# A sparse-attention kernel: turned blocks multiplied by diagonal matrices of reciprocals, a row test and one difference computed by GpSimd

## The chip, the cores and the metric

The kernel runs on one core of a Trainium2 chip. The time is that of one launch on the device in microseconds (us), the median of several runs. PE is TensorE, DVE is VectorE, ACT is ScalarE, POOL is GpSimd, and SP issues the transfers.

## The reference

Input `x` has 16 batches of 512 rows of 128. Each batch goes through attention with 16 heads and 16 extra memory keys, with the heads mixed before and after the softmax and only the 64 largest scores of each row kept, then through a gated feed-forward block. Each of the two has a layer norm ahead, one behind, and a residual addition.

```python
dots = jnp.einsum('bhid,bhjd->bhij', q, k) * scale
dots = jnp.einsum('bhij,hk->bkij', dots, pre_proj)
dots = jnp.where(causal[None, None], neg, dots)
vk = lax.top_k(dots, 64)[0][..., -1:]
dots = jnp.where(dots < vk, neg, dots)
attn = jax.nn.softmax(dots, axis=-1)
attn = jnp.einsum('bhij,hk->bkij', attn, post_proj)
out = jnp.einsum('bhij,bhjd->bhid', attn, v)
x = x + layernorm(out @ Wo + bo)
x = x + layernorm(ffn(layernorm(x)))   # ffn: (silu(x wg) * (x wu)) wd
```

## The kernel before

The weights are multiplied into each other at the start, so that a head needs a score product (`a_all`, `gT`) and a value product (`b_all`, `u_all`) and no output projection. Then one loop runs over the 16 batches and, within a batch, over 16 steps, one head each (`step(s)` on each engine; a first, seven times two middle ones, a last and a drain that finishes what is in flight). A head's 512 rows are four tiles `t` of 128 rows; because of the causal mask tile `t` has 128(t+1) keys, and 16 memory keys, so 144, 272, 400 and 528 columns (`ROW`), 1344 in all.

A head is spread over eight steps. In its own step PE makes the scores and DVE copies them with the row maxima (L1207). In the following steps the 64th largest value of each row is found by guesses: ACT counts per row how many scores lie above a guess (`signs`, L913, three guesses a step), and DVE turns the counts into new guesses (L1120 to L1146, "the moves"; `between` is the difference of two brackets, masked in L1128). Four steps on, DVE counts above the last guess (`found`, L1073), POOL subtracts what is above (L1355), DVE takes the eight largest of the rest (`max`, L1087), and `offset` (POOL, L1336: ranks plus `found`) picks the right one, reduced to `kth` (L1095). `spread` and `missed` (L1102, L1107) test whether the last guess was so far off that this doesn't hold for some row; PE sums `missed` over the rows into `flag_part`, DVE copies it to `flags` (L1070), and where it is above zero DVE does the slow selection `general_kth`. Six steps on, DVE makes `probs` (exponentials at or above `kth`, L1188) with their row sums and the reciprocals `rinv` (L1193), POOL multiplies `probs` by them (L1347) and copies the memory columns to `pmem` (L1362), PE turns the blocks of 128 x 128 (L783, ten a head), ACT copies them out (`probsT`, L924), and a step later PE multiplies them with the values into `y_bank` (L770).

The order on each engine is that of the code, written by hand; engines meet at semaphores. The waits that matter here: POOL's `offset` of a step waits for `kth` of the same step of DVE (`kth_ready`), because it overwrites what the reduce reads; POOL's scaling waits for `rinv` of the same step; PE's turning waits for `scaled`. Steps 1, 8, 9 and 15 have a layer norm on POOL behind `offset` (`extras`, L1256 to L1275), steps 0, 7, 8 and 14 its statistics on DVE behind L1207, step 10 maxima of memory scores, and steps 11 to 13 the gate of the feed-forward block (`f_up`) on DVE behind the moves.

## Time and profile before

| | |
|---|---|
| median of 3 runs | 3364.86 us (3363.4 to 3366.53) |
| the profiled execution | 3363.66 us, span 3361.9 us |
| its mean granted TensorE clock | 0.903 of 2.4 GHz |
| DVE, ACT busy | 88%, 86% of the span |
| PE, POOL busy | 80%, 56% |
| transfers | 22.66 MB, mean 7 GB/s |

The span is first to last instruction of the profiled execution. "Busy" counts instructions that compute, and one that overlaps the end of the one ahead is not counted twice in it. Where the profile gives the start of two instructions on one engine, their distance says what the first costs that engine, waits included; the duration also has the part that overlaps the next. A wait is put down to the instruction whose semaphore came last.

### The profile page before, as it was taken

To read this page: it belongs to the slowest core of one execution; us is meant where nothing else is said; L and a number is where in the kernel's file an instruction comes from. 1 tells how busy PE (TensorE), PEld (TensorE's weight loads), DVE (VectorE), ACT (ScalarE), POOL (GpSimd) and SP (SyncE) were. 2 spreads that over 40 slices of the span, in tenths; PEclk is the share of its full clock that TensorE was granted. 3 is DMA by queue.
4 is the path that set the end of the run, shared out by engine and by line. 5 is a ranking of instruction groups with operands and counts; after the bars stand their busy time and mean duration, and the time that the engine had idled before them with its cause. 6 is when DMAs were issued, how large, how long until landed. Compare 5 with 4: busy or idle time off the path is not lost. (4 is left out here: it accounts for less than half of the span.)

```text
span 3361.9 us, 70684 instructions
## 1 busy us (share of the span) xinstructions
PE 2675.5 (80%) x13754; PEld 1771.9 (53%) x13754; DVE 2958.5 (88%) x12547; ACT 2891.6 (86%) x8666; POOL 1887.2 (56%) x3623
## 2 busy tenths in 40 slices
PE   7878888888877888888787867887788887888765
PEld 3455555555545555555555545555455555555543
DVE  4599999999989999999999989998999999998985
ACT  1699989898978989999898978989899898989972
POOL 3455566555655555566565546655565665555543
PEclk8989899898988998999999888989899899999977
DMA  1000000000000000000000000000000000000000
GB/s 44 7 2 2 5 8 5 9 2 5 8 5 9 2 9 5 5 9 5 8 2 11 2 5 8 3 11 2 5 8 5 9 2 11 2 5 9 2 8 4
DMA packets 31404, 22.66 MB, mean 7 GB/s; under 512 B 3201, under 2 KB 30338, under 8 KB 30722
## 3 DMA queue, kind: packets, MB, share of 16 engines
q1 hardware_dynamic: 30722, 16.03, 1.7%
q14 instruction: 555, 4.55, 0.4%
q8 instruction: 127, 2.08, 0.3%
HBM read 11.83 MB, written 4.19 MB: 5 GB/s over the span
## 5 line engine op out<-in xcount | busy, mean ns | idle before, releaser
L913 ACT ACTIVATE signs<-scores,state 128x528 int8<-128x528 f32 (+3 forms) x3072 | 1723.5, 574 | 74.7 <-DVE state L1146 74.2
L1347 POOL TENSOR_SCALAR probs<-probs,rinv 128x528 f32<-128x528 f32 (+3 forms) x1024 | 538.9, 545 | 1300.6 <-DVE rinv L1193 1300.6
L783 PE MATMUL t_bank<-ident,probs 128*128 128x128 f32 x2560 | 485.5, 334 | 601.9 <-POOL probs L1347 593.6
L1355 POOL TENSOR_TENSOR work<-scores,work 128x528 f32<-128x528 f32 (+3 forms) x1024 | 888.3, 900 | 11.6 <-DVE work L1073 11.6
L759 PE MATMUL s_bank<-xn,gT 128*128 128x512 f32 (+3 forms) x2048 | 761.8, 496 | 1.8 <-ACT gT L844 0.7
L783 PEld LDWEIGHTS t_bank<-ident,probs 128*128 128x128 f32 x2560 | 325.7, 164 | 708.6 <-issue 582.5
L770 PEld LDWEIGHTS y_bank<-u_all,probsT 128*128 128x128 f32 x5120 | 616.8, 194 | 109.4 <-issue 98.8
L770 PE MATMUL y_bank<-u_all,probsT 128*128 128x128 f32 x5120 | 625.4, 278 | 6.6 <-ACT probsT L924 6.5
L924 ACT COPY probsT<-t_bank 128x512 f32<-128x512 f32 (+1 forms) x768 | 400.5, 522 | 251.2 <-PE t_bank L783 247.6
L913 ACT ACTIVATION_READ_ACCUMULATOR signs<-scores,state 128x1 f32 x3072 | 614.7, 200 | 0.0
L1073 DVE TENSOR_SCALAR_CACHE_REDUCE work<-scores,state 128x528 f32<-128x528 f32 (+3 forms) x1024 | 531.1, 553 | 46.2 <-DVE state L1146 46.2
L934 ACT ACTIVATE expo<-scores,negmax 128x528 f32<-128x528 f32 (+3 forms) x1024 | 542.2, 590 | 0.0
L1188 DVE SCALAR_TENSOR_TENSOR probs<-scores,kth,expo 128x528 f32<-128x528 f32 (+3 forms) x1024 | 520.9, 565 | 9.1 <-issue 6.1
L1207 DVE TENSOR_SCALAR_CACHE_REDUCE scores<-s_bank,memmax 128x512 f32<-128x512 f32 (+3 forms) x1024 | 516.5, 543 | 5.9 <-PE s_bank L761 5.7
L759 PEld LDWEIGHTS s_bank<-xn,gT 128*128 128x128 f32 x2048 | 358.1, 210 | 286.2 <-issue 276.2
L1087 DVE MAX8 state<-work 128x8 f32<-128x528 f32 (+3 forms) x1024 | 441.5, 491 | 0.2 <-issue 0.2
L631 PE MATMUL misc<-b_all,xn 128*128 128x512 f32 x512 | 301.4, 673 | 9.2 <-ACT u_all L844 9.2
L668 PE MATMUL misc<-xn,a_all 128*128 128x512 f32 x512 | 264.3, 598 | 6.0 <-DVE f_up L1162 6.0
L761 PE MATMUL s_bank<-causal,ident 128*128 128x128 bf16 x1024 | 228.5, 223 | 0.0
L761 PEld LDWEIGHTS s_bank<-causal,ident 128*128 128x128 bf16 x1024 | 105.7, 103 | 128.2 <-issue 91.0
L844 ACT COPY u_all<-misc 128x512 f32<-128x512 f32 x256 | 148.9, 582 | 8.5 <-PE misc L631 8.5
L844 ACT COPY gT<-misc 128x512 f32<-128x512 f32 x256 | 151.8, 593 | 0.9 <-PE misc L668 0.9
(156 smaller groups left out, 2984.0 us busy)
## 6 DMA issues: line engine op xcount, KB each, us to landing
xwork<-in_L_attn_x_dram SPq DMA_DIRECT2D x17, 256.0 KB, 2.8
xres<-in_L_attn_x_dram SPq DMA_DIRECT2D x16, 256.0 KB, 2.9
out_dram<-ybuf SPq DMA_DIRECT2D x16, 256.0 KB, 2.4
u_all<-in_L_attn_Wq_dram SPq DMA_DIRECT2D x1, 512.0 KB, 3.5
u_all<-in_L_attn_Wk_dram SPq DMA_DIRECT2D x1, 512.0 KB, 4.4
u_all<-in_L_attn_Wv_dram SPq DMA_DIRECT2D x1, 512.0 KB, 5.3
u_all<-in_L_attn_Wo_dram SPq DMA_DIRECT2D x1, 512.0 KB
expo<-in_L_ffn_w_gate_dram SPq DMA_DIRECT2D x1, 192.0 KB, 4.7
```

Source lines behind the costliest of these rows:

```text
L759: nc.tensor.matmul(score_part(t, 0, KEYS[t]), lhsT=gT[s % 2][:, t * P:(t + 1) * P], rhs=xn[par][:, 0:KEYS[t]], start=True, stop=False, ski ...
L770: mm = nc.tensor.matmul(y_bank[:, t * P:(t + 1) * P], lhsT=probsT[:, h % 2, at:at + P], rhs=u_all[:, j, h * D:(h + 1) * D], start=False, s ...
L783: mm = nc.tensor.transpose(t_bank[q % 2][:, at:at + P], probs[:, h % 2, KEY_AT[t] + j * P:KEY_AT[t] + (j + 1) * P], ident[:, :])
L913: nc.scalar.activation(signs[:, k, AT[t]:AT[t] + ROW[t]], row(scores, ring(head_of(s, k + 1), RING), t), ACT.Sign, bias=guesses(s % STATES ...
L924: nc.scalar.copy(probsT[:, h % 2, PART_AT[q]:PART_AT[q + 1]], t_bank[q % 2][:, 0:PART_AT[q + 1] - PART_AT[q]]).then_inc(t_taken, 1)
L934: nc.scalar.activation(row(expo, ring(head_of(s, LAG_E), ERING), t), row(scores, ring(head_of(s, LAG_E), RING), t), ACT.Exp, bias=negmax[: ...
L1073: v.tensor_scalar(work[:, s % 2, AT[t]:AT[t] + ROW[t]], row(scores, slot_k, t), guessed[:, t:t + 1], None, ALU.is_ge, ALU.add, accum_out=f ...
L1087: v.max(candidates(past)[:, t, 1:9], work[:, s % 2, AT[t]:AT[t] + ROW[t]]).then_inc(select_step, 1)
L1188: v.scalar_tensor_tensor(out=probs[:, slot_p % 2, AT[t]:AT[t] + ROW[t]], in0=row(scores, slot_p, t), scalar=kth[:, bass.ds(slot_p, 1), t], ...
L1207: v.tensor_scalar(keys(scores, slot, t), score_part(t, 0, KEYS[t]), 1.0, memmax[par][:, t, bass.ds(s, 1)], ALU.mult, ALU.max, accum_out=ro ...
L1347: nc.gpsimd.tensor_scalar(prb, prb, rinv[:, slot_p, t:t + 1], 1.0, ALU.mult, ALU.mult).then_inc(scaled, 1)
L1355: nc.gpsimd.tensor_tensor(wrk, row(scores, slot_k, t), wrk, ALU.subtract).then_inc(hidden, 1)
```

## The change

Four things change.

- POOL no longer multiplies `probs` by `rinv`. It multiplies the identity by it, one 128 x 128 matrix `diag[:, t, :]` for each tile, and PE's turn becomes a real matrix product with that diagonal as moving operand, which turns and scales the block at once. `pmem` gets its factor in POOL's copy, now a multiplication with two inputs. The scaling waits for PE's previous turn (`t_full`).
- `spread` and `missed` are made by POOL, from two more columns of `offset` (11 for each tile, `found` less the aim plus and minus the reach), as a product and a comparison with 0. DVE's two instructions go.
- The sum of `missed` over the tiles is no longer made with `missed`; DVE's copy of `flags` adds up instead (an instruction with an accumulator).
- The bracket difference `between` is made by POOL at the end of these, and DVE waits for it (`between_ready`) ahead of L1128.

```diff
@@ PE, turn @@
-                        mm = nc.tensor.transpose(t_bank[q % 2][:, at:at + P],
-                                                 probs[:, h % 2, KEY_AT[t] + j * P:KEY_AT[t] + (j + 1) * P], ident[:, :])
+                        mm = nc.tensor.matmul(t_bank[q % 2][:, at:at + P],
+                                              lhsT=probs[:, h % 2, KEY_AT[t] + j * P:KEY_AT[t] + (j + 1) * P],
+                                              rhs=diag[:, t, :], start=True, stop=True, skip_group_check=True)
@@ DVE @@
-                        v.tensor_copy(flags[:, :], flag_part).then_inc(flag_taken, 1)
+                        v.tensor_scalar(flags[:, 0:T], flag_part, 1.0, None, ALU.mult, ALU.add,
+                                        accum_out=flags[:, T:T + 1]).then_inc(flag_taken, 1)
...
-                    if checks:
-                        number = found[:, (s - 1) % 2, :]
-                        dve.wait_ge(found_ready, 4 * ge + 4)
-                        alone(dve)
-                        v.scalar_tensor_tensor(out=spread[:, :], in0=number, scalar=-2.0 * AIM, in1=number,
-                                               op0=ALU.add, op1=ALU.mult).then_inc(select_step, 1)
-                        dve.wait_ge(select_step, 1)
-                        at_least(dve, flag_full, ge)
-                        alone(dve)
-                        v.scalar_tensor_tensor(out=missed[:, 0:T], in0=spread[:, :], scalar=WINDOW ** 2 + 0.5 - AIM ** 2,
-                                               in1=active, op0=ALU.is_gt, op1=ALU.mult,
-                                               accum_out=missed[:, T:T + 1]).then_inc(bad_ready, 1)
...
-                        v.tensor_tensor(between[:, :, :], pair(past, S_T, -1), pair(last, S_OTHER, 0),
-                                        ALU.subtract).then_inc(guess_step, 1)
...
+                        dve.wait_ge(guess_step, 2)
+                        dve.wait_ge(between_ready, g - 1)
+                        alone(dve)
                         v.scalar_tensor_tensor(out=between[:, :, :],
@@ POOL @@
-                        nc.gpsimd.tensor_tensor(offset[:, :, 0:9], ranks,
-                                                found[:, (s - 1) % 2, :].unsqueeze(2).to_broadcast([P, T, 9]),
+                        nc.gpsimd.tensor_tensor(offset[:, :, 0:11], ranks,
+                                                found[:, (s - 1) % 2, :].unsqueeze(2).to_broadcast([P, T, 11]),
                                                 ALU.add).then_inc(offset_ready, 1)
+                        ge = g - LAG_E
+                        pool.wait_ge(offset_ready, ge + 1)
+                        alone(pool)
+                        nc.gpsimd.tensor_tensor(spread[:, :], offset[:, :, 0:1].squeeze(2), offset[:, :, 1:2].squeeze(2),
+                                                ALU.mult).then_inc(spread_ready, 1)
+                        pool.wait_ge(spread_ready, ge + 1)
+                        at_least(pool, flag_full, ge)
+                        alone(pool)
+                        nc.gpsimd.tensor_scalar(missed[:, :], spread[:, :], 0.0, 1.0, ALU.is_gt, ALU.mult).then_inc(bad_ready, 1)
+                    if any(lagged(kind, s, k + 2) for k in range(GUESSES)):
+                        last, past = (s - 1) % STATES, (s - 2) % STATES
+                        at_least(pool, guess_ready, g - 2)
+                        at_least(pool, first_ready, g - 1 if lagged(kind, s, 2) else 0)
+                        alone(pool)
+                        nc.gpsimd.tensor_tensor(between[:, :, :], pair(past, S_T, -1), pair(last, S_OTHER, 0),
+                                                ALU.subtract).then_inc(between_ready, 1)
                     extras(kind, b, s)
                     gp, slot_p = g - LAG_P, head_of(s, LAG_P) % 2
                     if lagged(kind, s, LAG_P):
                         pool.wait_ge(rinv_ready, gp + 1)
                         at_least(pool, probs_ready, 4 * gp + 4)
+                        at_least(pool, t_full, 3 * gp)
                         alone(pool)
                         for t in SCORE_ORDER:
-                            prb = probs[:, slot_p, AT[t]:AT[t] + ROW[t]]
-                            nc.gpsimd.tensor_scalar(prb, prb, rinv[:, slot_p, t:t + 1], 1.0, ALU.mult,
+                            nc.gpsimd.tensor_scalar(diag[:, t, :], ident[:, :], rinv[:, slot_p, t:t + 1], 1.0, ALU.mult,
                                                     ALU.mult).then_inc(scaled, 1)
...
-                        pool.wait_ge(scaled, 4 * gp + 4)
                         alone(pool)
-
-                        nc.gpsimd.tensor_copy(head_mem(pmem, head_of(s, LAG_P)), mem_parts(probs[:, slot_p, :])).then_inc(pmem_ready, 1)
+                        shares = rinv[:, slot_p, :].rearrange("p (a t) -> p a t", a=2).unsqueeze(3)
+                        nc.gpsimd.tensor_tensor(head_mem(pmem, head_of(s, LAG_P)).rearrange("p a t m -> p a t m"),
+                                                mem_parts(probs[:, slot_p, :]), shares.to_broadcast([P, 2, 2, M]),
+                                                ALU.mult).then_inc(pmem_ready, 1)
```

On POOL, from the last subtraction of one step to the scaling of the next, in a middle batch. Before:

```order
L1355 TENSOR_TENSOR work<-scores,work 128x144 [waits found_ready]
L1362 COPY pmem<-probs 128x4x16 [waits scaled]
L1312 ISA
L1315 TENSOR_TENSOR negmax<-rowmax,minus_unit 128x4 [waits masked]
L1321 COPY state<-seed 128x2x4 [waits guess_ready]
L1330 COPY scores<-smem 128x2x32 [waits probs_ready]
L1336 TENSOR_TENSOR offset<-consts,found 128x4x9 [waits kth_ready,found_ready]
L1347 TENSOR_SCALAR probs<-probs,rinv 128x528 [waits rinv_ready,probs_ready]
```

And now, the same place:

```order
L1365 TENSOR_TENSOR work<-scores,work 128x144 [waits found_ready]
L1371 TENSOR_TENSOR pmem<-probs,rinv 128x4x16
L1306 ISA
L1309 TENSOR_TENSOR negmax<-rowmax,minus_unit 128x4 [waits masked]
L1315 COPY state<-seed 128x2x4 [waits guess_ready]
L1324 COPY scores<-smem 128x2x32 [waits probs_ready]
L1330 TENSOR_TENSOR offset<-consts,found 128x4x11 [waits kth_ready,found_ready]
L1336 TENSOR_TENSOR spread<-offset 128x4 [waits offset_ready]
L1341 TENSOR_SCALAR missed<-spread 128x4 [waits spread_ready,flag_full]
L1347 TENSOR_TENSOR between<-state 128x24 [waits guess_ready,first_ready]
L278 REGISTER_ALU [waits probs_ready,rinv_ready]
L1357 TENSOR_SCALAR diag<-ident,rinv 128x128 [waits t_full]
```

Three instructions stand between `offset` and the scaling that did not stand there, two of them behind waits for the one ahead, and `between` is the last of them.

On DVE, from the choice of the 64th value to the masked bracket, same batch. Before:

```order
L1090 SCALAR_TENSOR_TENSOR offset<-offset,state 128x4x9 [waits select_step,offset_ready]
L1094 ISA [waits select_step]
L1095 TENSOR_REDUCE kth<-offset 128x4
L1102 SCALAR_TENSOR_TENSOR spread<-found 128x4 [waits found_ready]
L1107 SCALAR_TENSOR_TENSOR missed<-spread,consts 128x4 [waits select_step,flag_full]
L1120 TENSOR_TENSOR state<-counts,consts 128x12 [waits first_ready,counted2,counted0,counted1]
L1121 TENSOR_TENSOR between<-state 128x24
L1125 TENSOR_TENSOR product<-state 128x24 [waits guess_step]
L1128 SCALAR_TENSOR_TENSOR between<-product,between 128x24 [waits guess_step]
```

And now:

```order
L1097 SCALAR_TENSOR_TENSOR offset<-offset,state 128x4x9 [waits select_step,offset_ready]
L1101 ISA [waits select_step]
L1102 TENSOR_REDUCE kth<-offset 128x4
L1114 TENSOR_TENSOR state<-counts,consts 128x12 [waits first_ready,counted2,counted0,counted1]
L1117 TENSOR_TENSOR product<-state 128x24 [waits guess_step]
L1122 SCALAR_TENSOR_TENSOR between<-product,between 128x24 [waits guess_step,between_ready]
```

Three instructions are gone between `kth` and the masked bracket, and the latter waits for POOL too.

## Rows read from the trace of the kernel before

**Rows 1.** The page, first part: engine busy us, share, instructions.

```profile
PE 2675.5 (80%) x13754; PEld 1771.9 (53%) x13754; DVE 2958.5 (88%) x12547; ACT 2891.6 (86%) x8666; POOL 1887.2 (56%) x3623
```

**Rows 2.** Who waited for whom: engine, line, releaser, us in total, times, longest.

```profile
POOL probs L1347 <- DVE rinv L1193: 1300.6, 256, 23.0
```

**Rows 3.** DVE in order of time: start us, us, engine, line, operation.

```profile
1515.12 0.18 DVE L1193 RECIPROCAL rinv<-rowsum 128x4 f32<-128x4 f32 x1
...
1520.08 0.20 DVE L1095 TENSOR_REDUCE kth<-offset 128x4 f32<-128x40 f32 x1
1520.19 0.41 DVE L1102 SCALAR_TENSOR_TENSOR spread<-found 128x4 f32<-128x4 f32 x1
...
1521.01 0.23 DVE L1120 TENSOR_TENSOR state<-counts,consts 128x12 f32<-128x12 f32 x1
...
1521.32 0.21 DVE L1125 TENSOR_TENSOR product<-state 128x24 f32<-128x24 f32 x1
1521.56 0.18 DVE L1128 SCALAR_TENSOR_TENSOR between<-product,between 128x24 f32<-128x24 f32 x1
...
1522.84 0.17 DVE L1146 TENSOR_TENSOR state<-state,move 128x12 f32<-128x12 f32 x1
...
1526.49 0.18 DVE L1193 RECIPROCAL rinv<-rowsum 128x4 f32<-128x4 f32 x1
```

**Rows 4.** POOL in order of time, the same step.

```profile
1515.50 2.10 POOL L1347 TENSOR_SCALAR probs<-probs,rinv 128x528 f32<-128x528 f32 x4 [4.91 <-DVE rinv L1193]
1517.57 3.46 POOL L1355 TENSOR_TENSOR work<-scores,work 128x528 f32<-128x528 f32 x4
1520.97 0.24 POOL L1362 COPY pmem<-probs 128x64 f32<-128x64 f32 x1
1521.16 0.20 POOL L1315 TENSOR_TENSOR negmax<-rowmax,minus_unit 128x4 f32<-128x4 f32 x1
...
1521.62 0.25 POOL L1336 TENSOR_TENSOR offset<-consts,found 128x36 f32<-128x36 f32 x1
```

**Rows 5.** Groups by form (POOL) and by line (DVE): count, busy us, mean ns.

```profile
L1347 POOL TENSOR_SCALAR probs<-probs,rinv 128x528 f32<-128x528 f32 x256 | 180.6, 705 | 1300.6 <-DVE rinv L1193 1300.6
...
L1355 POOL TENSOR_TENSOR work<-scores,work 128x144 f32<-128x144 f32 x256 | 125.5, 490 | 0.0
L1347 POOL TENSOR_SCALAR probs<-probs,rinv 128x144 f32<-128x144 f32 x256 | 98.5, 385 | 0.0
...
L1121 DVE TENSOR_TENSOR between<-state 128x24 f32<-128x24 f32 x258 | 53.2, 206 | 0.2 <-issue 0.2
```

**Rows 6.** A step with a normalization, in order of time: DVE, then POOL.

```profile
1644.56 0.20 DVE L1095 TENSOR_REDUCE kth<-offset 128x4 f32<-128x40 f32 x1
...
1645.66 0.22 DVE L1128 SCALAR_TENSOR_TENSOR between<-product,between 128x24 f32<-128x24 f32 x1
...
1646.95 0.95 DVE L1146 TENSOR_TENSOR state<-state,move 128x12 f32<-128x12 f32 x1
...
1649.31 0.77 DVE L1188 SCALAR_TENSOR_TENSOR probs<-scores,kth,expo 128x528 f32<-128x528 f32 x1
...
1644.92 0.24 POOL L1336 TENSOR_TENSOR offset<-consts,found 128x36 f32<-128x36 f32 x1
1645.26 0.25 POOL L1256 TENSOR_SCALAR vareps<-meanvar 128x4 f32<-128x4 f32 x1
1645.65 1.04 POOL L1259 TENSOR_TENSOR rstd<-vareps,minus_half 128x4 f32<-128x4 f32 x1
1646.84 1.04 POOL L1268 TENSOR_TENSOR ybuf<-ybuf,rstd 128x512 f32<-128x512 f32 x1
1648.02 0.73 POOL L1274 TENSOR_TENSOR ybuf<-xres,ybuf 128x256 f32<-128x256 f32 x1
```

**Rows 7.** PE in order of time: products into `y_bank`, then turned blocks.

```profile
1499.29 2.39 PE L770 MATMUL y_bank<-u_all,probsT 128*128 128x128 f32 x20
...
1504.99 0.65 PE L783 MATMUL t_bank<-ident,probs 128*128 128x128 f32 x4 [2.33 <-POOL probs L1347]
```

More of the change, by code:

```diff
@@ L139, in guess_table @@
             table[i, T + t] = (z - FAR / (2 * density)) * UNIT ** 0.5
-            table[i, 5 * T + 9 * T + t] = float(active)
-            table[i, 5 * T + 10 * T + t] = 0.0 if active else -FMAX
+            reach = WINDOW + 0.5 if active else FAR
+            table[i, 5 * T + 11 * t] = reach - AIM
+            table[i, 5 * T + 11 * t + 1] = -reach - AIM
+            table[i, 5 * T + 11 * T + t] = 0.0 if active else -FMAX
         for k in range(GUESSES):
             table[:, 2 * T + k * T + t] = ROW[t] - 2 * AIM - 0.25
-        table[:, 5 * T + 9 * t:5 * T + 9 * t + 9] = np.arange(9) - TOPK
+        table[:, 5 * T + 11 * t + 2:5 * T + 11 * t + 11] = np.arange(9) - TOPK
     return table
@@ L324, in build @@
         centre = sb("centre", [P, P])
+        diag = sb("diag", [P, T, P])
         row_sum = sb("row_sum", [P, 2 * HC])
@@ L342, in build @@
         found = sb("found", [P, 2, T])
-        offset = sb("offset", [P, T, 10])
+        offset = sb("offset", [P, T, 12])
         spread = sb("spread", [P, T])
-        missed = sb("missed", [P, T + 1])
+        missed = sb("missed", [P, T])
         flags = sb("flags", [1, T + 1])
@@ L443, in build @@
         select_step = sem("select_step")
+        spread_ready = sem("spread_ready")
         bad_ready = sem("bad_ready")
+        between_ready = sem("between_ready")
         scaled = sem("scaled")
@@ L1053, in _ @@
             dve.wait_ge(state_set, 3)
-            nc.vector.tensor_copy(offset[:, :, 9:10].squeeze(2), cap)
+            nc.vector.tensor_copy(offset[:, :, 11:12].squeeze(2), cap)
             def batch(kind, b, par):
@@ L1088, in step @@
                         dve.wait_ge(offset_ready, gp + 1)
-                        dve.wait_ge(select_step, T + 1)
-                        v.scalar_tensor_tensor(out=offset[:, :, 0:9], in0=offset[:, :, 0:9], scalar=0.0,
+                        dve.wait_ge(select_step, T)
+                        v.scalar_tensor_tensor(out=offset[:, :, 2:11], in0=offset[:, :, 2:11], scalar=0.0,
                                                in1=candidates(past), op0=ALU.is_equal,
                                                op1=ALU.mult).then_inc(select_step, 1)
-                        dve.wait_ge(select_step, T + 2)
+                        dve.wait_ge(select_step, T + 1)
                         dve.sem_clear(select_step)
-                        v.tensor_reduce(kth[:, bass.ds(slot_p, 1), :].squeeze(1), offset[:, :, :], AX_X,
+                        v.tensor_reduce(kth[:, bass.ds(slot_p, 1), :].squeeze(1), offset[:, :, 2:12], AX_X,
                                         ALU.add).then_inc(kth_ready, 1)
-                    if checks:
-                        number = found[:, (s - 1) % 2, :]
-                        dve.wait_ge(found_ready, 4 * ge + 4)
-                        alone(dve)
-                        v.scalar_tensor_tensor(out=spread[:, :], in0=number, scalar=-2.0 * AIM, in1=number,
-                                               op0=ALU.add, op1=ALU.mult).then_inc(select_step, 1)
-                        dve.wait_ge(select_step, 1)
-                        at_least(dve, flag_full, ge)
-                        alone(dve)
-                        v.scalar_tensor_tensor(out=missed[:, 0:T], in0=spread[:, :], scalar=WINDOW ** 2 + 0.5 - AIM ** 2,
-                                               in1=active, op0=ALU.is_gt, op1=ALU.mult,
-                                               accum_out=missed[:, T:T + 1]).then_inc(bad_ready, 1)
                     if moves:
@@ L1134, in step @@
                                                in1=miss, op0=ALU.is_gt, op1=ALU.mult).then_inc(guess_step, 1)
-                        dve.wait_ge(guess_step, 4)
+                        dve.wait_ge(guess_step, 3)
                         v.tensor_tensor(other, pair(last, S_OTHER, 0), between[:, :, :], ALU.add).then_inc(guess_step, 1)
+                        dve.wait_ge(guess_step, 5)
+                        v.tensor_tensor(apart[:, :, :], pair(last, S_T, 0), other, ALU.subtract).then_inc(guess_step, 1)
                         dve.wait_ge(guess_step, 6)
-                        v.tensor_tensor(apart[:, :, :], pair(last, S_T, 0), other, ALU.subtract).then_inc(guess_step, 1)
-                        dve.wait_ge(guess_step, 7)
                         v.reciprocal(apart[:, 1, :], apart[:, 1, :]).then_inc(guess_step, 1)
                         v.tensor_tensor(move[:, :], apart[:, 0, :], move[:, :], ALU.mult).then_inc(guess_step, 1)
+                        dve.wait_ge(guess_step, 8)
+                        v.tensor_tensor(move[:, :], move[:, :], apart[:, 1, :], ALU.mult).then_inc(guess_step, 1)
                         dve.wait_ge(guess_step, 9)
-                        v.tensor_tensor(move[:, :], move[:, :], apart[:, 1, :], ALU.mult).then_inc(guess_step, 1)
-                        dve.wait_ge(guess_step, 10)
                         dve.sem_clear(guess_step)
```

11 lines of the change are left out of this document (5 added, 6 removed).

## Prediction

> **What bounds the kernel now.** I read the busy shares first, then the waits, then one step of each engine in order of time. The shares [rows 1] put DVE (VectorE) at 88% and ACT (ScalarE) at 86%, POOL (GpSimd) at 56%, PE (TensorE) at 80%. The largest wait is POOL's, for DVE's reciprocals `rinv`, 1300.6 us in 256 times, about 5 us in every step [rows 2]; none of DVE's own waits is among the long ones. So a step is as long as DVE's chain, with ACT close behind: it gains room if DVE's steps get longer, and would hold DVE back soon if they got shorter.
>
> The step that I use runs from `rinv` at 1515.12 to `rinv` at 1526.49, 11.37 us [rows 3]. Three stretches make it up: `rinv` to the reduce that gives `kth` 4.96 (1520.08), `kth` to L1128 1.48 (1521.56), L1128 to the next `rinv` 4.93. POOL's side of that step [rows 4]: it starts 0.38 behind `rinv` (1515.50), scales for 2.07, subtracts (L1355) for 3.40, copies `pmem` 0.19, and reaches `offset` 0.46 after `negmax`, at 1521.62, which is `rinv` + 6.50. It then idles until the next `rinv`.
>
> **What leaves DVE.** `spread` and `missed` go: from `kth` to L1120 it is 0.93 (1520.08 to 1521.01) [rows 3]. `kth` to `spread`, with one pair of waits between, is 0.11; L1120 has one pair more, so I take 0.23 for what stays, a gain of 0.70. `between` (L1121) goes too, but it stood in the shadow of the result that L1125 needs: L1120 to L1125 is 0.31, a dependent pair (L1125 to L1128) 0.24, so about 0.07. The new wait in front of L1128 costs about 0.1, the distance that a further wait takes in front of L1120. `flags` becomes an instruction with an accumulator; the bounds are 0 and 0.24, a dependent pair; I take 0.1, since the old copy and the new one have equally few columns. DVE by itself would gain 0.70 + 0.07 - 0.1 - 0.1, about 0.57 a step. That is what the change is worth if nobody is late.
>
> **What POOL gets, and when.** The place decides. `between` of a step stands on POOL behind `offset`, `spread` and `missed` of the same step, and `offset` waits for `kth` of the same step, since it overwrites what the reduce reads. DVE would come to L1128 at `kth` + 0.79. On the old timing POOL reaches only `offset` at `kth` + 1.54. So DVE will wait there, and POOL's queue is on the path. Its time, from `rinv`:
> - start 0.38.
> - four diagonal blocks of 128 columns in place of 1344 columns. The 528-column form takes 705 ns, the 144-column one 385 [rows 5], 0.83 ns a column; of the 2.07 for all four that leaves 0.24 each, so a block of 128 costs 0.35, the four 1.38. The bounds are 0.24 and 0.39 each. Gain only 0.69, because most of a short instruction is fixed.
> - L1355 unchanged, 3.40.
> - `pmem` with a second input, 64 columns: between the copy's 0.19 and the 0.49 of L1355's 144-column form [rows 5]; I take 0.28, near `offset` (36 columns, 0.25).
> - `negmax` to `offset` 0.46.
>
> `offset` then starts at 0.38 + 1.38 + 3.40 + 0.28 + 0.46 = 5.90. The other bound is DVE: where POOL had to wait for `kth`, `offset` came 0.36 behind it (1644.56, 1644.92) [rows 6], here 4.96 + 0.1 + 0.36 = 5.42. The later one counts, 5.90.
>
> Behind it three more instructions, two of which read the result of the one ahead. The row for such a pair is `vareps` to `rstd`: 0.39 for an instruction of 0.25 [rows 6], so its duration plus 0.14. `offset` 0.27 + 0.14 = 0.41; `spread` as `negmax`, 0.20 + 0.14 and 0.04 for a second wait, 0.38; `missed` to `between` between 0.14 (`negmax` to the next) and 0.34 (`offset` to `vareps`), I take 0.23; `between` 0.23 + 0.14 until DVE goes on, 0.37. Sum 1.39. L1128 starts at `rinv` + 7.29; now it is 6.44. With 4.93 behind it the step is 12.22: **0.85 longer**.
>
> **Two opinions on small work on POOL.** DVE's `between` takes 206 ns [rows 5], POOL's nearest row, `offset` with more columns, 0.25 us. The Trainium skill, page "GPSIMD Engine Reference", section "Engine selection", speaks against this move: elementwise work belongs on VectorE, GpSimd being about twice as slow on two inputs. By that factor, an estimate, `between` on POOL would take 0.41 instead of 0.23 and the whole kernel 46 us more. The rows say that at these sizes the factor is near 1.2, and that place and dependence cost more than the engine's speed.
>
> **The other steps.** A batch has 16 steps. In 11 of them nothing but the above lies between `rinv` and `kth` (with the three that work on `f_up`, which lies elsewhere): 11 x 0.85 = 9.4. In five, DVE has statistics or maxima there, and `kth` is so late that POOL waits for it even today: L1128 comes at `kth` + 0.1 + 0.36 + 1.39 = 1.85, where it was 1.10 (1644.56 to 1645.66) [rows 6]: +0.75. In one (maxima) that is all. In the four whose POOL has a normalization there, a stall goes: L1146 took 0.95 there and 0.17 otherwise, because it ran into POOL's `ybuf` instruction of 1.04 (from 1646.84, `offset` + 1.92). After the change POOL's follows `between` by the same 1.92, L1146 by 0.37 + 1.29 = 1.66, in time. So -0.78. But L1188 then starts at `between` + 3.24 (1646.95 to 1649.31 less the stall is 1.58), into POOL's next instruction, which begins at +3.10: until about 3.7 where it has 256 columns (0.73; two steps), about 4.0 where 512 (1.04; one step). Together 4 x (0.75 - 0.78) + 2 x 0.45 + 0.75 = 1.5. A batch is longer by 9.4 + 0.75 + 1.5 = 11.6, sixteen batches by **186 us**. The profiled execution took 3363.66 (span 3361.9), 1.2 below the median of the three runs; 3363.66 + 186 = 3550, on the median's scale 3551.
>
> **PE and ACT.** A turned block was one matmul; a real product of this type is two: ten blocks of `y_bank` are 20 in 2.39, 0.12 each, four turned ones were 4 in 0.65 [rows 7]. So ten more, 1.2 us a step. Cover: PE was idle for 2.33 before the first turned block, which is more than 1.2. It may also begin 0.33 earlier, as the first block to wait for costs POOL 0.37 (385 less 16 columns) and no longer 0.70; its first four blocks then take 8 x 0.12 = 0.96 and no longer 0.65. ACT, which copies them out, gets them within 0.1 of the old time and has gained 0.85 of room. Price 0; if the cover is gone, as where PE's granted clock is at its lower level, the first four blocks come later by their growth, up to 0.3 a step, 77 us.
>
> **Rivals.**
> - POOL's queue is cheaper than I make it, and only `kth` rules it: `offset` at 5.42, L1128 at 6.81, +0.37 in the 11 steps; 4.1 + 0.75 + 1.5 = 6.3 a batch, +101: 3465. For it: several short instructions are priced from neighbours. Against it: 0.48 us would have to be found in 1.66 of them (the blocks and `pmem`), and their fixed part alone is 1.1.
> - DVE's gain arrives: `between` would have to be ready by `kth` + 0.79, while `kth` + 0.36 + 1.39 is the earliest with every price above. It decides at 1.0 us less, as if POOL did the difference ahead of `offset`. Then 0.57 x 256 = 146 off: 3218. For it: `between` needs nothing from `kth`. Against it: the order of POOL's instructions.
> - It cancels: the wait costs just DVE's gain, 3365. It would need L1128 near `kth` + 1.4, below the same 1.75.
> - PE and ACT come on top: 3550 + 77 = 3627. For it: ACT at 86% and twice the instructions in front of its copies. Against it: the cover above.
>
> **How the numbers follow.** Forecast 0.74, the cheaper queue 0.12, PE and ACT on top 0.08, cancelling 0.02, faster 0.04. A measurement tells 0.2% of this kernel (7 us) from no change. Slower 0.94, same 0.02, faster 0.04. The range takes the two neighbours, 3465 to 3627; the unknown prices (0.11 for the distance to `between`, 0.06 for the blocks, 0.1 for the added wait for `t_full`) make 0.27 a step, 69 us, and stay within it.
>
> **What would show it.** After: POOL's wait for `rinv` still about 5 us a step (4.93 + 0.14 + 0.38 less `between`), so nothing of it is won; a wait of DVE at the masked `between` for POOL's, in nearly every step, of 7.29 - 4.96 - 0.1 - 0.79 = 1.4 us where POOL's queue rules and 1.0 where `kth` does, some 300 us in all; DVE's busy share falling; steps of 12.2. No such wait, or steps under 11.37, makes the prediction wrong; a wait of about 1.0 with steps of 11.7 makes it the cheaper queue.

## The result, and the profile of the changed kernel

| kernel | median us | lowest to highest | ratio to before |
|---|---|---|---|
| before | 3364.19 | 3363.4 to 3366.53 | 1 |
| changed | 3548.22 | 3544.98 to 3551.0 | 1.0545 [1.0527, 1.0564] |

The change costs 184 us; 3551 (3465 to 3627) was predicted. The profiled execution of the changed kernel took 3544.98 us, its span is 3543.2. The page, first part, and then the waits (engine, line, releaser, us in total, times, longest):

```profile
PE 2902.9 (82%) x16314; PEld 2152.0 (61%) x16314; DVE 2808.3 (79%) x11777; ACT 2903.2 (82%) x8666; POOL 1914.3 (54%) x4393
```

```profile
POOL diag L1357 <- DVE rinv L1187: 1339.7, 256, 22.8
...
DVE between L1122 <- POOL between L1347: 356.5, 255, 2.0
...
POOL offset L1330 <- DVE kth L1102: 45.8, 75, 2.2
```

DVE fell from 88% [rows 1] to 79%, and a wait that was not there, of 356.5 us in 255 steps, stands in front of the masked `between`. POOL idles for `rinv` as long as before (1339.7; 1300.6 in [rows 2]). Each engine now waits for the other once a step. DVE in order of time, in the step that answers to [rows 3]:

```profile
1501.02 0.18 DVE L1187 RECIPROCAL rinv<-rowsum 128x4 f32<-128x4 f32 x1
...
1505.60 0.34 DVE L1097 SCALAR_TENSOR_TENSOR offset<-offset,state 128x36 f32<-128x36 f32 x1
1506.07 0.20 DVE L1102 TENSOR_REDUCE kth<-offset 128x4 f32<-128x40 f32 x1
1506.30 0.28 DVE L1114 TENSOR_TENSOR state<-counts,consts 128x12 f32<-128x12 f32 x1
1506.61 0.18 DVE L1117 TENSOR_TENSOR product<-state 128x24 f32<-128x24 f32 x1
1508.32 0.18 DVE L1122 SCALAR_TENSOR_TENSOR between<-product,between 128x24 f32<-128x24 f32 x1 [1.53 <-POOL between L1347]
...
1513.22 0.18 DVE L1187 RECIPROCAL rinv<-rowsum 128x4 f32<-128x4 f32 x1
```

POOL in the same step, to be set beside [rows 4]:

```profile
1501.45 1.41 POOL L1357 TENSOR_SCALAR diag<-ident,rinv 128x128 f32<-128x128 f32 x4 [7.18 <-DVE rinv L1187]
1502.82 3.48 POOL L1365 TENSOR_TENSOR work<-scores,work 128x528 f32<-128x528 f32 x4
1506.26 0.29 POOL L1371 TENSOR_TENSOR pmem<-probs,rinv 128x64 f32<-128x64 f32 x1
1506.51 0.19 POOL L1309 TENSOR_TENSOR negmax<-rowmax,minus_unit 128x4 f32<-128x4 f32 x1
...
1506.99 0.26 POOL L1330 TENSOR_TENSOR offset<-consts,found 128x44 f32<-128x44 f32 x1
1507.39 0.20 POOL L1336 TENSOR_TENSOR spread<-offset 128x4 f32<-128x4 f32 x1
1507.78 0.24 POOL L1341 TENSOR_SCALAR missed<-spread 128x4 f32<-128x4 f32 x1 [0.19 <-POOL spread L1336]
1507.99 0.24 POOL L1347 TENSOR_TENSOR between<-state 128x24 f32<-128x24 f32 x1
```

DVE has its product at 1506.61 and could go on at about 1506.9. POOL reaches `offset` at 1506.99 and needs 1.24 more until `between` is done. DVE goes on at 1508.32, which is `rinv` + 7.30. The step is 12.20 long, where it was 11.37.

### The profile page after: what moved, and what is told of

Read it like the earlier page. It is cut to its first block and busy times, and to the rows that moved or that the text cites. A ratio compares the mean times of both kernels' runs of the same rounds, so it can differ in the third digit from the quotient of the medians.

```text
span 3543.2 us, 76572 instructions
## 1 busy us (share of the span) xinstructions
PE 2902.9 (82%) x16314; PEld 2152.0 (61%) x16314; DVE 2808.3 (79%) x11777; ACT 2903.2 (82%) x8666; POOL 1914.3 (54%) x4393
## 5 line engine op out<-in xcount | busy, mean ns | idle before, releaser
L788 PE MATMUL t_bank<-diag,probs 128*128 128x128 f32 x5120 | 841.8, 334 | 553.2 <-POOL diag L1357 547.9
L788 PEld LDWEIGHTS t_bank<-diag,probs 128*128 128x128 f32 x5120 | 781.2, 240 | 582.7 <-issue 486.6
L1357 POOL TENSOR_SCALAR diag<-ident,rinv 128x128 f32<-128x128 f32 x1024 | 362.5, 374 | 1341.2 <-DVE rinv L1187 1339.7
L764 PE MATMUL s_bank<-xn,gT 128*128 128x512 f32 (+3 forms) x2048 | 688.8, 458 | 0.8 <-ACT gT L850 0.7
L775 PE MATMUL y_bank<-u_all,probsT 128*128 128x128 f32 x5120 | 617.5, 276 | 5.4 <-ACT probsT L930 5.3
L919 ACT ACTIVATION_READ_ACCUMULATOR signs<-scores,state 128x1 f32 x3072 | 601.0, 196 | 0.0
L1182 DVE SCALAR_TENSOR_TENSOR probs<-scores,kth,expo 128x528 f32<-128x528 f32 (+3 forms) x1024 | 554.5, 597 | 26.9 <-issue 18.7
L764 PEld LDWEIGHTS s_bank<-xn,gT 128*128 128x128 f32 x2048 | 329.9, 195 | 238.1 <-issue 230.2
L1122 DVE SCALAR_TENSOR_TENSOR between<-product,between 128x24 f32<-128x24 f32 x258 | 49.1, 190 | 356.9 <-POOL between L1347 356.5
L636 PE MATMUL misc<-b_all,xn 128*128 128x512 f32 x512 | 283.9, 637 | 9.4 <-ACT u_all L850 9.4
```

The lines of the kernel that those rows point to most:

```text
L764: nc.tensor.matmul(score_part(t, 0, KEYS[t]), lhsT=gT[s % 2][:, t * P:(t + 1) * P], rhs=xn[par][:, 0:KEYS[t]], start=True, stop=False, ski ...
L775: mm = nc.tensor.matmul(y_bank[:, t * P:(t + 1) * P], lhsT=probsT[:, h % 2, at:at + P], rhs=u_all[:, j, h * D:(h + 1) * D], start=False, s ...
L788: mm = nc.tensor.matmul(t_bank[q % 2][:, at:at + P], lhsT=probs[:, h % 2, KEY_AT[t] + j * P:KEY_AT[t] + (j + 1) * P], rhs=diag[:, t, :], s ...
L919: nc.scalar.activation(signs[:, k, AT[t]:AT[t] + ROW[t]], row(scores, ring(head_of(s, k + 1), RING), t), ACT.Sign, bias=guesses(s % STATES ...
L1182: v.scalar_tensor_tensor(out=probs[:, slot_p % 2, AT[t]:AT[t] + ROW[t]], in0=row(scores, slot_p, t), scalar=kth[:, bass.ds(slot_p, 1), t], ...
L1357: nc.gpsimd.tensor_scalar(diag[:, t, :], ident[:, :], rinv[:, slot_p, t:t + 1], 1.0, ALU.mult, ALU.mult).then_inc(scaled, 1)
```

## Experiments

In what follows a plain step is one without statistics or maxima ahead of `kth`. Its length is read from two `rinv` rows. Where I give the length of a kind of step over all batches, it is the median over the batches of the distance between two successive `rinv` rows. The experiments ran in three groups, each beside runs of the kernel before of its own (median 3364.42 for e1 to e4, 3359.99 for e5 to e8, 3368.55 for e9 and e10; 3364.19 beside the changed kernel). Where two kernels of different groups are compared, the difference of the ratios is the safer one, and it is given where it differs.

Theory: each part of the change does for DVE what it is meant to do, and the loss comes only from the order on POOL's queue: `offset`, `spread`, `missed` and only then `between`, with DVE waiting for the last. Rivals: each part is slow by itself on POOL; or PE and ACT, with twice the instructions in front of the copies of the turned blocks, hold the step.

### One part at a time

**e1_diag.** The kernel before with the diagonal matrices alone:

```
-  mm = nc.tensor.transpose(t_bank[...], probs[...], ident[:, :])
+  mm = nc.tensor.matmul(t_bank[...], lhsT=probs[...], rhs=diag[:, t, :], ...)
...
-  nc.gpsimd.tensor_scalar(prb, prb, rinv[:, slot_p, t:t + 1], 1.0, ...)
+  nc.gpsimd.tensor_scalar(diag[:, t, :], ident[:, :], rinv[:, slot_p, t:t + 1], 1.0, ...)
...
-  nc.gpsimd.tensor_copy(head_mem(pmem, ...), mem_parts(probs[...]))
+  nc.gpsimd.tensor_tensor(head_mem(pmem, ...), mem_parts(probs[...]), shares..., ALU.mult)
```

> The kernel before with the first part alone: diagonal matrices on POOL, real products on PE, the scaled copy of pmem. The row test and the bracket difference stay on DVE. Theory (the change is slow because DVE waits for POOL's bracket difference): no DVE instruction waits for POOL here, so no loss; POOL's subtraction ends about 0.7 us earlier in a step, so that DVE's spread and missed, stretched to 0.41 and 0.32 beside it in the rows of before, run at 0.16 and 0.22 as in the steps with a normalization: 0.2 to 0.3 us a step less, 3300 to 3355. Rival (the real products cost twice PE's instructions and hold ACT and DVE back): slower than before by up to 0.7 us a step, 3400 to 3545.

Measured: 3321.96 us (3321.17 to 3323.16) beside 3364.42 of before, ratio 0.9869 [0.9853, 0.9886]: 42 us faster, as the theory expected. The plain step is 11.07. Two rows of DVE and one of POOL tell where the gain is:

```profile
1507.88 0.20 DVE L1097 TENSOR_REDUCE kth<-offset 128x4 f32<-128x40 f32 x1
1508.00 0.16 DVE L1104 SCALAR_TENSOR_TENSOR spread<-found 128x4 f32<-128x4 f32 x1
...
1508.07 0.30 POOL L1363 TENSOR_TENSOR pmem<-probs,rinv 128x64 f32<-128x64 f32 x1
```

`spread` takes 0.16 here and took 0.41 in [rows 3]. There POOL's subtractions (from 1517.57 for 3.46, to 1521.03 [rows 4]) still ran when it started at 1520.19. Here POOL's queue is 0.6 us earlier: the last subtraction gives way to `pmem` at 1508.07, 0.07 behind the start of `spread`, and leaves it next to nothing to wait for. The parts of the change touch each other through this: the diagonal matrices give DVE time, though they take nothing off it.

**e2_test.** The kernel before with the row test alone on POOL (table, `offset` with 44 columns, `flags` with an accumulator):

```
-  v.scalar_tensor_tensor(out=spread[:, :], ...)
-  v.scalar_tensor_tensor(out=missed[:, 0:T], ..., accum_out=missed[:, T:T + 1])
...
+  nc.gpsimd.tensor_tensor(spread[:, :], offset[:, :, 0:1]..., offset[:, :, 1:2]..., ALU.mult)
+  nc.gpsimd.tensor_scalar(missed[:, :], spread[:, :], 0.0, 1.0, ALU.is_gt, ALU.mult)
```

> The kernel before with the row test alone moved to POOL (spread and missed behind offset, the sum made by DVE's copy of flags). Theory: nothing on DVE waits for POOL's test, so DVE keeps its gain as far as POOL's subtraction, which now runs beside the moves, and ACT's load let it: between 3240 and 3330. Rival (a longer POOL queue or the accumulating flags copy is what costs): slower than before, above 3375.

Measured: 3299.85 us (3294.62 to 3301.94), ratio 0.9799 [0.978, 0.9818], 65 us faster and within what was expected; DVE does not wait for POOL.

**e3_between.** The kernel before with the difference alone on POOL, right behind `offset`:

```
-  v.tensor_tensor(between[:, :, :], pair(past, S_T, -1), pair(last, S_OTHER, 0), ALU.subtract)
...
+  dve.wait_ge(between_ready, g - 1)
...
+  nc.gpsimd.tensor_tensor(between[:, :, :], pair(past, S_T, -1), pair(last, S_OTHER, 0),
+                          ALU.subtract).then_inc(between_ready, 1)
```

> The kernel before with the bracket difference alone moved to POOL, behind offset, and the wait for it on DVE. Theory: offset starts at rinv + 6.50 as before, the difference 0.33 later, DVE goes on 0.37 after that, at 7.20 where it was 6.44: 0.76 us in 11 of 16 steps, none in the others: 3365 + 134, about 3500 (3460 to 3530), with a DVE wait of 200 us or more at the masked bracket. Rival (the products are the cause): within 20 us of before.

Measured: 3440.82 us (3437.22 to 3442.61), ratio 1.0221 [1.0203, 1.0239]: 76 us slower. The sign is as expected, the size about half, and the time lies below the 3460 to 3530 that were expected. One plain step, DVE and then POOL:

```profile
1526.90 0.20 DVE L1096 TENSOR_REDUCE kth<-offset 128x4 f32<-128x40 f32 x1
...
1528.10 0.26 DVE L1124 TENSOR_TENSOR product<-state 128x24 f32<-128x24 f32 x1
1528.98 0.18 DVE L1129 SCALAR_TENSOR_TENSOR between<-product,between 128x24 f32<-128x24 f32 x1 [0.63 <-POOL between L1345]
...
1528.44 0.25 POOL L1337 TENSOR_TENSOR offset<-consts,found 128x36 f32<-128x36 f32 x1
1528.65 0.25 POOL L1345 TENSOR_TENSOR between<-state 128x24 f32<-128x24 f32 x1
```

I had put 0.33 between `offset` and `between`, the price where the next instruction needs the one ahead; `between` needs nothing of `offset`, and it is 0.21. The steps with a normalization gained besides, since the stall of L1146 [rows 6] went there.

By themselves the three parts give -42, -65 and +76, together -31. The change gives +184. So no part explains the loss by its own cost: 215 us come only when the three are together. That it is their order on POOL's queue, the next runs show.

### The change without the moved difference, and with it elsewhere

**e4_diag_test.** The changed kernel with the difference back on DVE, so the first two parts together:

```
+  v.tensor_tensor(between[:, :, :], pair(past, S_T, -1), pair(last, S_OTHER, 0), ALU.subtract)
...
-  dve.wait_ge(between_ready, g - 1)
...
-  nc.gpsimd.tensor_tensor(between[:, :, :], ...).then_inc(between_ready, 1)
```

> The changed kernel with the bracket difference alone given back to DVE; everything else of the change stays. Theory: the wait goes, DVE gains what its own chain lost, 0.5 us a step less what ACT allows (its own work is about 11.2 us in a step with two extras): 3215 to 3290. Rival (products on PE and ACT cost the time): stays above 3450.

Measured: 3277.58 us (3275.49 to 3281.39), ratio 0.9739 [0.9721, 0.9756]. It beats both kernels, the one before by 87 us. A plain step, DVE and POOL's `offset`:

```profile
1535.97 0.18 DVE L1186 RECIPROCAL rinv<-rowsum 128x4 f32<-128x4 f32 x1
...
1541.04 0.20 DVE L1101 TENSOR_REDUCE kth<-offset 128x4 f32<-128x40 f32 x1
...
1541.80 0.24 DVE L1121 SCALAR_TENSOR_TENSOR between<-product,between 128x24 f32<-128x24 f32 x1
...
1546.79 0.18 DVE L1186 RECIPROCAL rinv<-rowsum 128x4 f32<-128x4 f32 x1
...
1541.97 0.28 POOL L1329 TENSOR_TENSOR offset<-consts,found 128x44 f32<-128x44 f32 x1
```

The masked `between` stands at `rinv` + 5.83, even ahead of POOL's `offset`; in the changed kernel it is at 7.30. The step is 10.82. Moving this one instruction of 206 ns [rows 5] costs the kernel 271 us.

**e5_early.** The changed kernel, POOL's `between` for the next step made right behind the diagonal matrices and ahead of the subtraction; no instruction more or less:

```
   nc.gpsimd.tensor_scalar(diag[:, t, :], ...)
+  nc.gpsimd.tensor_tensor(between[:, :, :], pair(prev, S_T, -1), pair(nxt, S_OTHER, 0),
+                          ALU.subtract).then_inc(between_ready, 1)
   ...
   nc.gpsimd.tensor_tensor(wrk, row(scores, slot_k, t), wrk, ALU.subtract)
```

> The changed kernel with one thing moved: POOL makes the bracket difference of the next step right behind the four diagonal blocks, ahead of its subtraction, in place of behind the row test. Same instructions, same count. Theory (place in POOL's queue and the dependence on kth cost the time, not POOL's speed): DVE finds it ready, waits under 10 us in all, and the time falls to that of the kernel with the difference on DVE (3278), within 3265 to 3310. Rival (POOL is simply given too much): stays above 3400.

Measured: 3309.81 us (3304.45 to 3315.69) beside 3359.99 of before, ratio 0.9852 [0.9835, 0.987]. The place of the instruction alone is worth 238 us (233 by the ratios). DVE no longer waits for it:

```profile
1500.83 0.53 DVE L1097 SCALAR_TENSOR_TENSOR offset<-offset,state 128x36 f32<-128x36 f32 x1
1501.49 0.20 DVE L1102 TENSOR_REDUCE kth<-offset 128x4 f32<-128x40 f32 x1
...
1502.04 0.18 DVE L1117 TENSOR_TENSOR product<-state 128x24 f32<-128x24 f32 x1
1502.36 0.18 DVE L1122 SCALAR_TENSOR_TENSOR between<-product,between 128x24 f32<-128x24 f32 x1
```

But it is still 32 us behind e4, which makes the difference on DVE, and 38 by the ratios (0.9852 against 0.9739). From `kth` to the masked `between` it is 0.87 here and 0.76 in e4: the wait costs more than the instruction in the shadow saved. And L1097 takes 0.53 here; the last two experiments are about that.

**e6_swap.** The changed kernel with `between` right behind `offset` and the test behind it:

```
   nc.gpsimd.tensor_tensor(offset[:, :, 0:11], ranks, ...)
+  nc.gpsimd.tensor_tensor(between[:, :, :], ...).then_inc(between_ready, 1)
   nc.gpsimd.tensor_tensor(spread[:, :], ...)
   nc.gpsimd.tensor_scalar(missed[:, :], ...)
-  nc.gpsimd.tensor_tensor(between[:, :, :], ...).then_inc(between_ready, 1)
```

> The changed kernel with the bracket difference right behind offset and the row test behind it: the dependence on kth stays, the two instructions of the test leave the path. Theory: offset at rinv + 5.96, the difference 0.20 later, DVE 0.34 after: L1122 at 6.5 where the changed kernel has 7.3, the kernel before 6.4, so plain steps of about 11.4: 3320 to 3385. Rival (the wait for kth in itself is what costs): above 3450.

Measured: 3363.01 us (3356.79 to 3365.93), ratio 1.0006 [0.9996, 1.0015]: no difference from before. Two instructions of 0.20 and 0.24 us and their waits, put behind `between` and not ahead of it, are worth 185 us (181 by the ratios):

```profile
1504.20 0.20 DVE L1102 TENSOR_REDUCE kth<-offset 128x4 f32<-128x40 f32 x1
...
1505.67 0.18 DVE L1122 SCALAR_TENSOR_TENSOR between<-product,between 128x24 f32<-128x24 f32 x1 [0.74 <-POOL between L1338]
...
1505.12 0.25 POOL L1330 TENSOR_TENSOR offset<-consts,found 128x44 f32<-128x44 f32 x1
1505.34 0.23 POOL L1338 TENSOR_TENSOR between<-state 128x24 f32<-128x24 f32 x1
```

The wait is halved, from 1.53 to 0.74. The three places of one instruction give 3548, 3363 and 3310: the theory of the order holds.

### The rival of PE and ACT

**e7_half.** The changed kernel, but PE turns the blocks with the identity as in before; the diagonal matrices are made and not used, so the scaling is left out of the result.

```
-  mm = nc.tensor.matmul(t_bank[...], lhsT=probs[...], rhs=diag[:, t, :], ...)
+  mm = nc.tensor.transpose(t_bank[...], probs[...], ident[:, :])
```

> The changed kernel with PE turning the blocks by the identity again, one instruction a block in place of two; the scaling by the reciprocals is left out of the result, all waits and POOL's diagonal blocks stay. Theory: PE's added 1.2 us a step lie in its idle time, the time stays within 20 us below 3548. Rival (the real products take part of the 184 us through ACT's copies): below 3500.

**e8_early_half.** The same edit in e5, where no wait for POOL covers PE; here too the scaling is left out of the result.

> The kernel with the early difference (e5), with PE turning by the identity again, the scaling left out of the result. Where DVE no longer waits for POOL, ACT and PE are close to being the bound (step 7 of a batch takes 15.8 us with the difference on DVE, DVE waiting 2.5 us for PE's flags). Theory: here the products cost something, 20 to 60 us less without them, 3225 to 3285. If the products are hidden here too: within 10 us of e5.

Measured: e7 3536.15 us (3533.12 to 3537.57), ratio 1.0524 [1.0506, 1.0541], 12 less than the changed kernel, but only 7 by the ratios, whose intervals overlap; e8 3295.17 (3293.26 to 3298.06), 15 less than e5, which ran beside it. e8 falls between what was expected by the two theories, so PE's instructions do cost something, but little. The waits of ACT for the turned blocks, changed kernel and then e7:

```profile
ACT probsT L930 <- PE t_bank L788: 448.9, 335, 19.3
```

```profile
ACT probsT L929 <- PE t_bank L788: 278.9, 191, 18.3
```

The doubled instructions make ACT wait 170 us more at this place, and at most 12 us of it reach the time: ACT waits for DVE's guesses instead (L918 of e7, 197.7 us, 53.0 in the changed kernel). With real products on PE the rival accounts for at most 12 of 184 us. What the doubled products would cost at an equal clock is not shown, since e7's granted clock is lower too (0.887 against 0.916).

### What is left between e4 and e5

VectorE's first SCALAR_TENSOR_TENSOR of the selection (`offset`, 36 columns) takes different times in different kernels, though it reads and writes the same. Where POOL is idle, as in the step with the first normalization, it takes 0.23 (the 0.16 in the texts below, written before the runs, is that of 4-column instructions). The theory: an instruction of DVE with two inputs in SBUF waits until POOL's running instruction with two inputs ends. The rival: the two share the port word by word, and it is just slower beside POOL.

**e9_order_a** and **e10_order_b.** e4 with POOL's four subtractions in another order:

```
-  for p, t in enumerate(ORDER):               # rows of 528, 400, 272, 144
+  for p, t in enumerate([3, 2, 0, 1]):        # e9:  528, 400, 144, 272
+  for p, t in enumerate([3, 1, 0, 2]):        # e10: 528, 272, 144, 400
```

The waits for DVE's counts `found` go with the rows: in e9 POOL's third subtraction waits for all four counts, in e10 its second. That moves nothing by itself: in the median of the plain steps the second subtraction starts at about 3.07 behind `rinv` in all three kernels, and the third at about 4.06 in e9 as in e4.

> The kernel without the moved difference (diagonal matrices and row test, 3277.6 us), with the last two of GpSimd's four subtractions exchanged: row lengths 528, 400, 144, 272 in place of 528, 400, 272, 144. Same instructions, same sum. In that kernel VectorE's first SCALAR_TENSOR_TENSOR of the selection comes to its turn 4.58 us behind `rinv` and takes 0.49 where it takes 0.16 alone; GpSimd's third subtraction ends 4.93, its fourth 5.39, and VectorE's next two-input instruction starts 5.43. Theory (VectorE's two-input instruction waits for the end of GpSimd's running one, whole): the third now ends 4.67, so the first one takes about 0.25 and `kth` comes about 0.25 earlier, but the next two-input instruction would then come at about 5.2 and waits for the end of the fourth, still 5.39. Net gain 0 to 0.1 a step: 3250 to 3280. Rival (the long duration comes from sharing a port word by word, or from something else): nothing changes place, 3277 within 5.

> As the run before, with the row lengths in the order 528, 272, 144, 400. Theory (whole-instruction wait): the third subtraction ends 4.40, the fourth runs from there to 5.39 and VectorE's SCALAR_TENSOR_TENSOR, due at 4.58, stands until its end, 0.98 in place of 0.49. `kth` is then about 0.4 later and nothing gives it back but the next two-input instruction, which no longer waits (0.05): about +0.35 in the 11 plain steps of a batch, less or nothing in the five where statistics or maxima push the instruction past GpSimd's end: +60, 3320 to 3350. Rival: no change, 3277 within 5.

Measured beside 3368.55 of before: e9 3309.58 us (3308.27 to 3311.2), ratio 0.9831 [0.9815, 0.9847]; e10 3299.88 (3296.38 to 3302.64), ratio 0.9803 [0.9785, 0.9821]. The groups by form of that instruction (times, busy us, mean ns) in e4, e5, e9 and e10:

```profile
L1096 DVE SCALAR_TENSOR_TENSOR offset<-offset,state 128x36 f32<-128x36 f32 x256 | 81.0, 316 | 28.6
```

```profile
L1097 DVE SCALAR_TENSOR_TENSOR offset<-offset,state 128x36 f32<-128x36 f32 x256 | 116.2, 454 | 28.6
```

```profile
L1096 DVE SCALAR_TENSOR_TENSOR offset<-offset,state 128x36 f32<-128x36 f32 x256 | 155.7, 608 | 28.6
```

```profile
L1096 DVE SCALAR_TENSOR_TENSOR offset<-offset,state 128x36 f32<-128x36 f32 x256 | 160.0, 625 | 28.6
```

A reordering on POOL of the same four instructions doubles the time of an instruction on DVE, from 316 to 608 and 625 ns. The rival, by which nothing would change, falls. Both of my expectations were missed all the same. For e9 the sign was wrong. I had taken POOL's times as means of one step of the batch that has two forms in e4: in seven batches POOL starts 0.42 behind `rinv` there, in seven 0.73. The mean, 0.58, fits neither of them, and in nearly all other steps POOL starts at 0.42 or 0.43. So the fourth subtraction begins at 4.51, just before DVE comes at 4.58, and DVE stands until that one gives way, as it does in e10. That the miss is explained by a start 0.15 earlier speaks for a wait of whole instructions. So do the two forms themselves: in the same kernel, with the same order on POOL, DVE's instruction takes 0.33 where POOL starts at 0.42, and 0.64 where POOL starts at 0.73. And so does where the stall ends. In the profiled executions of before, the changed kernel, e4, e5, e9 and e10, DVE's instruction ends 0.12 to 0.14 behind the start of POOL's next one, in the median of the plain steps, at whatever length that makes it: 0.27, 0.33, 0.34, 0.53, 0.78, 0.79.

e10 was expected 60 us slower than e4, and is 22 slower. Its plain steps are 0.27 longer (11.07 and 10.80), not 0.35, and one step of the batch is shorter by 1.7, as in e9.

Of the two sizes, 292 ns more in the mean of 256 steps would be 75 us in e9, and the time rose by 32. Part comes back at L1113, which no longer meets POOL (237 ns in the mean in e4, 178 in e9: 15 us). Another part is one kind of step, the one with the first normalization, which is 15.8 long in e4 and 14.2 in e9: in e4 DVE stands 2.59 in front of `flags` there, for a product of PE that is queued behind others. Over 16 batches that is 26 us. What makes PE late in just this step of e4 was not tried; a kernel with e4's parts and without that wait is the next thing to look for. These pieces are read from single profiles and don't add up exactly.

## Why the prediction was right, step by step

**POOL's queue rules, and its sum.** In the step shown, from `rinv`, with the predicted value in brackets: first diagonal matrix 0.43 (0.38); four of them 1.37 (1.38); subtraction 3.44 (3.40); `pmem` 0.25 (0.28); `negmax` to `offset` 0.48 (0.46), so `offset` at 5.97 (5.90). Then `spread` behind `offset` 0.40 (0.41), `missed` 0.39 (0.38), `between` 0.21 (0.23), DVE goes on after 0.33 (0.37): 7.30 (7.29). To the next `rinv` 4.90 (4.93), the step 12.20 (12.22). Two small misses cancel: the wait for `t_full` takes 0.05 at the start, which I had kept only in the range, and the handing over from POOL to DVE is 0.04 cheaper than a dependent pair on POOL with its duration.

**DVE's side.** `kth` came at 5.05, by the prediction 5.06. But for another reason: the accumulator in `flags` costs nothing (`flags` is followed by the next instruction after 0.08, as in before), and L1097 is 0.07 longer because it meets POOL's subtraction at another place. `kth` to L1114 is 0.23, as taken. The wait at L1122 is 356.5 us in 255 steps; "some 300 us" was forecast. POOL's own wait for `rinv`, 1339.7 us or 5.2 a step, is as forecast.

**The other steps.** The medians of the 16 kinds of steps make a batch 11.7 longer, 11.6 predicted. Inside it the pieces differ: the 11 steps 9.8 (9.4), one by one between 0.58 and 1.16 (0.85 each); the one with the maxima 0.54 (0.75); the four with a normalization together 1.35 (1.5), one by one 0.42, 0.58 (0.42 for each of these), 0.46 (0.72) and -0.12 (-0.03). (The step with the maxima is itself one of the three that work on `f_up`, so the 11 hold two of these, not three as the prediction says.) Here is one of the four, DVE and then POOL, which answers to [rows 6]:

```profile
1729.59 0.21 DVE L1122 SCALAR_TENSOR_TENSOR between<-product,between 128x24 f32<-128x24 f32 x1 [1.04 <-POOL between L1347]
1730.87 0.17 DVE L1140 TENSOR_TENSOR state<-state,move 128x12 f32<-128x12 f32 x1
...
1732.45 1.18 DVE L1182 SCALAR_TENSOR_TENSOR probs<-scores,kth,expo 128x528 f32<-128x528 f32 x1
1733.56 1.08 DVE L1182 SCALAR_TENSOR_TENSOR probs<-scores,kth,expo 128x400 f32<-128x400 f32 x1
...
1729.97 1.04 POOL L1253 TENSOR_TENSOR rstd<-vareps,minus_half 128x4 f32<-128x4 f32 x1
1731.15 1.04 POOL L1262 TENSOR_TENSOR ybuf<-ybuf,rstd 128x512 f32<-128x512 f32 x1
1732.34 0.72 POOL L1268 TENSOR_TENSOR ybuf<-xres,ybuf 128x256 f32<-128x256 f32 x1
1733.02 1.19 POOL L1269 TENSOR_TENSOR ybuf<-xres,ybuf 128x256 f32<-128x256 f32 x1
```

The stall of 0.95 at the last instruction of the bracket [rows 6] is gone (0.17), since DVE passes 0.28 before `ybuf` begins. It comes back where the prediction put it, at L1182, which starts 0.11 behind the start of POOL's addition. What I had missed is the second stall: the 400-column one takes 1.08, and POOL's second addition 1.19 where the first takes 0.72. The two engines block each other in turn. The prediction priced one stall of 0.45 and there are two, of 0.41 and 0.45. That the sum still came out is luck: other pieces of these steps are shorter than assumed, and what the normalization and maxima steps fall short of the forecast, the 11 others make up.

**PE and ACT** at price 0: 7 to 12 us by e7. The 77 us for a lost cover were not reached.

**The opinion of the notes on small work.** The Trainium skill, page "GPSIMD Engine Reference", section "Engine selection", makes GpSimd about twice as slow on two inputs, which would have given 46 us more. POOL's `between` takes 239 ns in the mean of 258 here, DVE's took 206 [rows 5], a factor of 1.16. At 24 columns the trace doesn't bear the factor out, and the nearest row did better than the rule. What made the place expensive is not the engine's speed: the same instruction on the same engine gives 3310, 3363 or 3548.

**A rival that was priced wrong.** "DVE's gain arrives", with POOL doing the difference ahead of `offset`, was put at 3218 us, 0.57 off in each of the 256 steps. e5 is that kernel, and it takes 3310. What failed there is 0.57 as the gain of every one of the 256 steps. In a plain step DVE gains 0.61 between `kth` and the masked `between` (0.87, where it was 1.48 [rows 3]), but `kth` comes 0.28 later (5.24 behind `rinv` in the median, where it was 4.96), because L1097 now waits for POOL's subtraction: 11.06, a gain of 0.31. And the four steps with a normalization gain only 0.2 together in a batch, where 2.3 was priced. I had weighed such collisions only for the case that I forecast.

## What to carry to other kernels

Work that moves to another engine is priced by what stands ahead of it in that engine's queue when the result is wanted, not by its duration: 0.2 us of work cost 271 us because it was queued behind all that POOL has to do in the step. Some 185 of them came from two small instructions ahead of it that could as well have stood behind (e6). If it must move and its inputs are there early, it goes ahead of that; and it is worth looking first whether it was in a shadow where it stood, for then the wait costs more than the instruction. Parts of a change that share a queue are to be tried apart: here two of three were good, and the two alone beat both kernels (3277.6 us, 2.6% under before).

## What the runs showed of the hardware

**DVE and POOL exclude each other by whole instructions.** An instruction of DVE with two inputs in SBUF, which takes 0.23 alone, took between 0.27 and 0.79 in the medians of six kernels, and ended 0.12 to 0.14 behind the start of POOL's next instruction each time. MAX8 and the reduce, with one input, keep their durations beside the same POOL instructions: in the kernel before, MAX8 of 528 columns takes 0.70 in the median beside a subtraction and 0.71 away from one, the reduce 0.195 both ways. The Trainium skill, page "SBUF — State Buffer", section "Who interferes with whom", says that the pair of ports which the two engines share is an exclusive lock, and that a DVE instruction with two inputs in SBUF contends with a GpSimd instruction that reads SBUF; e9 and e10 agree. The row above that does not fit it is `rstd`, two inputs of 4 columns, 1.04 us from 1729.97: DVE's L1140, which also has two inputs, starts at 1730.87 within it and takes 0.17. This is no single case: in the twelve profiled executions 1440 two-input instructions of DVE start with 0.2 us or more of `rstd` to run, and none is longer than usual by over 0.05; nor is any of the 367 that start so within `missed`, which has one input of 4 columns. So it is not simply every POOL instruction with two inputs that locks DVE out for as long as its record lasts; whether the columns or the operation decides was not tried.

**Small instructions on POOL have a floor.** A TENSOR_SCALAR of 128 columns is followed by the next after 0.35, of which 0.24 does not depend on the columns, an estimate from the two forms of L1347 in [rows 5]; one with 4 columns takes 0.24 (`missed`) or 0.20 (`spread`, a TENSOR_TENSOR), one with 24 (`between`) 0.24. A result handed to the next instruction on the same engine adds some 0.14.

**TensorE's clock rose with the real products.** The mean granted clock was 0.953 in e1, 0.957 in e4 and 0.952 in e5, and 0.911 in e2 and 0.910 in e8, which turn blocks with the identity; 0.916 in the changed kernel against 0.887 in e7, which differ in nothing else. The share is of 2.4 GHz, with the other level at 1.2. A faster clock could give back a part of what the doubled products cost PE; how much of it reached the time was not measured.
